# Second-choice result loads on ScalarE's DMA queue, first-choice loads on SyncE's

## The chip, the cores and the metric

The kernel runs on 1 core of one Trainium2 chip. The metric is the device time of one execution in microseconds, taken as the median of several runs. All times of the profile are of one profiled execution and count from the start of its span.

## What is computed

Two blocks over x of 8 x 512 tokens x 256 features, each an adaptively modulated attention followed by an adaptively modulated feed-forward part. The last of the four parts is a mixture of experts: every token picks 2 of 8 experts, each expert takes at most 1280 slots, and the two results of a token are added with its two shares. Cut to that part:

```python
top_p, top_i = jax.lax.top_k(probs, K)                      # K = 2
top_p = top_p / jnp.sum(top_p, axis=-1, keepdims=True)
...
fc1 = jax.nn.gelu(jnp.einsum('ech,ehf->ecf', xt, moe_w1))   # E = 8 experts, cap 1280
fc2 = jnp.einsum('ecf,efh->ech', fc1, moe_w2).reshape(T, H)
weighted = fc2 * padded_probs[:, None]
moe_out = jnp.zeros((N, H)).at[padded_tid].add(weighted)
return h1 + moe_out.reshape(S, B, H)
...
x = x + gb * _L1_ffn_ref(h, ...)
```

## The kernel before

Everything is written by hand in one stream per engine with semaphores between them; nothing is scheduled by a planner. `layer0`, `layer1` and `cross` compute the first three parts with x held in SBUF; `moe` is the last part and the only one that the change touches.

In `moe`, 40 chunks of 256 slots go through the experts. For each chunk GpSimd gathers rows (L2153), TensorE turns them and does both products (L2360, L2374, L2386), ScalarE applies the gain and the Gelu (L2313, L2321), VectorE copies the result out of PSUM (L2257), and GpSimd scatters it by indirect DMA (L2161) into the DRAM tensor `expert_parts` (`c.parts`). This tensor has two halves of 4096 rows of 256 floats: the results of the tokens' first choices, and those of the second.

After the last scatter the two halves are put together, one batch b = 0..7 of 512 tokens at a time:

- SyncE waits until the base sums are done and all four scatter semaphores are full (L2132 to L2135), and then issues 16 loads back to back, in the order y(0), rows(0), y(1), rows(1), ...: L2137 loads the first choices' results of batch b into `c.y[:, b]`, L2138 the second choices' into `rows(b)`, which lies in `c.prob` for b < 4 and in `c.probT` from there. Each is 512 KB, 128 partitions x 4 runs of 1 KB. Both raise `landed{b}`; batches 6 and 7 share one semaphore.
- Behind them in SyncE's stream stand 8 waits on `finished`, each with one store of a batch to the output (L2141).
- ScalarE waits for `landed{b}` and scales y(b) by the first share, in 4 ACTIVATEs (L2330), raising `scaled`.
- VectorE's `summed(b)` waits for `scaled` and adds rows(b) times the second share, 4 instructions at L2275; `finished(b)` multiplies by the gate (L2282) and adds to x (L2283). They are written in the order summed(0), summed(1), finished(0), summed(2), finished(1), ...

ScalarE's stream has no DMA in it anywhere in the program, and between its last Gelu (L2321) and its first scaling (L2330) it has nothing to do but wait.

Of the kernel before, what the change touches and what calls it, by code (L numbers as in the profile page):

```python
# [23 lines left out]
B = 8  # L24
T = 512
# [83 lines left out]
def mod_rows(c, l, name):  # L109

    at = CHUNK[name] * D
    return c.mod_dram[l, :, at:at + D].partition_broadcast(P)
# [1938 lines left out]
TT = CHUNK_T // P  # L2051
CHUNKS = CAP // CHUNK_T
ALL_CHUNKS = E * CHUNKS
# [4 lines left out]
BUFS = 4  # L2058
# [4 lines left out]
def moe(c, d, start, out):  # L2063

    nc = c.nc
    s = c.s
    with ExitStack() as st:
# [37 lines left out]
        def rows(b):  # L2105
            half = c.prob if b < B // 2 else c.probT
            at = 2 * (b % (B // 2))
            return half[:, at:at + 2, :].rearrange("p i (t n) -> p (i t) n", n=D)
# [4 lines left out]
        def tokens(dram, b):  # L2113
            return dram[b * T:(b + 1) * T, :].rearrange("(t p) n -> p t n", p=P)
# [7 lines left out]
        @block.sync  # L2122
        def _(sp):
            sp.dma_start(gate[:, :, :], mod_rows(c, 1, "gb")).then_inc(s["moe_loaded"], 16)
            for e in range(E):
                z = e % 2
                if e >= 2:
                    sp.wait_ge(s["down_full"], CHUNKS * (e - 1))
                sp.dma_start(w1[z][:, :, :], d["we1"][e].rearrange("(k p) n -> p k n", p=P))\
                  .then_inc(s[("expert_weights0", "expert_weights1")[z]], 16)  # L2130
                sp.dma_start(w2[z][:, :, :], d["we2"][e].rearrange("(k p) n -> p k n", p=P))\
                  .then_inc(s[("expert_weights0", "expert_weights1")[z]], 16)  # L2132
            sp.wait_ge(s["base_done"], B)
            for z in range(BUFS):
                sp.wait_ge(s[("scattered0", "scattered1", "scattered2", "scattered3")[z]], 16 * TT * (ALL_CHUNKS // BUFS))  # L2135
            for b in range(B):
                sp.dma_start(c.y[:, b], tokens(c.parts[0:B * T, :], b)).then_inc(s[f"landed{min(b, B - 2)}"], 16)  # L2137
                sp.dma_start(rows(b), tokens(c.parts[B * T:2 * B * T, :], b)).then_inc(s[f"landed{min(b, B - 2)}"], 16)  # L2138
            for b in range(B):
                sp.wait_ge(s["finished"], b + 1)  # L2140
                sp.dma_start(out[b].rearrange("(t p) n -> p t n", p=P), c.x[:, b]).then_inc(s["stored"], 16)  # L2141
            sp.wait_ge(s["stored"], 16 * B)
# [149 lines left out]
        @block.scalar  # L2292
        def _(act):
            act.wait_ge(s["logits_shifted"], 1)
            nc.scalar.activation(lg[:, :, :], lg[:, :, :], ACT.Exp).then_inc(s["logits_exped"], 1)

            act.wait_ge(s["lows_ready"], 1)
            for x in range(1, PAIRS // PIECE, 2):
                if x >= 2:
                    act.wait_ge(s["pairs_used"], x - 1)  # L2300
                for m in range(PIECE):
                    k = PIECE * x + m
                    ins = nc.scalar.activation(lohot[1][:, m, :], c.lows[:, 0, :], ACT.Abs, bias=minus_low[:, k:k + 1],  # L2303
                                               scale=1.0)
                ins.then_inc(s["low_away"], 1)
                act.wait_ge(s["low_away"], x // 2 + 1)
                nc.scalar.activation(lohot[1][:, :, :], lohot[1][:, :, :], ACT.Relu, bias=c.ones[:, 0:1], scale=-1.0)\  # L2307
                  .then_inc(s["low_hots"], 1)

            def gain(j):  # L2310
                act.wait_ge(s["in_full"], j + 1)
                for k in range(KD):
                    ins = nc.scalar.activation(inT[j % 2][:, k, :], IN[j % 2][:, k * CHUNK_T:(k + 1) * CHUNK_T],  # L2313
                                               ACT.Identity, bias=c.gains[:, 2 + k:3 + k], scale=c.gains[:, k:k + 1])
                ins.then_inc(s["in_out"], 1)

            gain(0)
            for j in range(ALL_CHUNKS):
                for i in range(2):
                    act.wait_ge(s["up_full"], 2 * j + i + 1)  # L2320
                    nc.scalar.activation(gT[j % 2][:, 2 * i:2 * i + 2, :],  # L2321
                                         UP[(2 * j + i) % 4].rearrange("p (m t) -> p m t", m=2),
                                         ACT.Gelu_apprx_tanh).then_inc(s["up_out"], 1)
                if j + 1 < ALL_CHUNKS:
                    gain(j + 1)
            for b in range(B):
                act.wait_ge(s[f"landed{min(b, B - 2)}"], 32 if b < B - 2 else 64)
                for t in range(NT):
                    k = b * NT + t
                    ins = nc.scalar.activation(c.y[:, b, t, :], c.y[:, b, t, :], ACT.Identity, bias=c.zero[:, :],  # L2330
                                               scale=share[:, 0, k:k + 1])
                ins.then_inc(s["scaled"], 1)
# [157 lines left out]
```

## Time and profile before

| | us |
|---|---|
| median of 3 runs | 3152.18 |
| lowest, highest | 3151.83, 3153.38 |
| the profiled execution's own time | 3159.02 |
| its span | 3157.3 |

| engine | busy us, share of the span |
|---|---|
| PE | 2904.5, 92% |
| DVE | 1646.8, 52% |
| ACT | 1403.8, 44% |
| POOL | 836.2, 26% |

The span runs from the first to the last instruction or transfer. PE's share is an average over the whole program; the last stretch, from 3107.7 us on, has no matmul in it, and there the shares of the table say nothing. Rows marked SPq are the DMA issues in SyncE's stream: start, and the time until the stream could go on.

### The profile page before, as it was taken

The numbers are of one execution on the slowest core, as the hardware profiler recorded it, in microseconds if no ns is written. First come the engines' busy times: TensorE is split into PE (matmuls) and PEld (weight loads), VectorE is DVE, ScalarE is ACT, GpSimd is POOL, SyncE is SP. The second block draws the span as 40 slices with busy tenths as digits, with TensorE's granted clock in tenths as the row PEclk, the third lists the DMA queues.
The fourth block names the chain that finished last, engine by engine and source line by source line (L and its number), as shares of the span: only waits on it lengthen the run. The fifth ranks groups of instructions, "written<-read, shape, count | busy, mean of one in ns | idle before, by whom it ended". The sixth has DMA issues, their size and how long they took to land. (4 is left out here: it accounts for less than half of the span.)

```text
span 3157.3 us, 53117 instructions
## 1 busy us (share of the span) xinstructions
PE 2904.5 (92%) x20820; PEld 1968.8 (62%) x20820; DVE 1646.8 (52%) x5006; ACT 1403.8 (44%) x3081; POOL 836.2 (26%) x831
## 2 busy tenths in 40 slices
PE   6889999878999999999999999999999688899993
PEld 3566666654666757576666666665656444478883
DVE  4667776645555544544444444445554488631114
ACT  3666666632535444444444444534444124132222
POOL 1001111113333332332323222233333311025551
PEclk8999999999999999999999999999999899789997
DMA  4111111004000000000010000000000000112325
GB/s 139 18 19 20 18 20 20 8 3 164 8 4 10 6 16 30 1 1 1 13 33 1 1 1 5 28 14 11 6 6 11 11 1 27 53 41 79 73 83 186
DMA packets 66232, 93.95 MB, mean 30 GB/s; under 512 B 9971, under 2 KB 52982, under 8 KB 64944
## 3 DMA queue, kind: packets, MB, share of 16 engines
q1 hardware_dynamic: 58304, 74.24, 8.0%
q0 software_dynamic: 7680, 16.32, 2.0%
q8 instruction: 166, 2.72, 0.4%
q14 instruction: 82, 0.67, 0.1%
HBM read 59.31 MB, written 27.36 MB: 27 GB/s over the span
## 5 line engine op out<-in xcount | busy, mean ns | idle before, releaser
L1343 PE MATMUL bank<-h2T,w 128*128 128x512 f32 x1024 | 478.9, 606 | 5.3 <-ACT gT L1281 3.7
L1381 PE MATMUL bank<-w,gT 128*128 128x256 f32 x2048 | 465.9, 381 | 0.0
L1381 PEld LDWEIGHTS bank<-w,gT 128*128 128x128 f32 x2048 | 379.3, 190 | 49.7 <-issue 0.5
L1018 POOL TENSOR_TENSOR prob<-prob,rsum 128x512 f32<-128x512 f32 (+1 forms) x256 | 237.7, 949 | 591.0 <-DVE rsum L1165 591.0
L1343 PEld LDWEIGHTS bank<-h2T,w 128*128 128x128 f32 x1024 | 182.2, 190 | 224.0 <-issue 173.7
L1281 ACT ACTIVATE gT<-bank,vec 128x512 f32<-128x512 f32 x256 | 175.1, 687 | 285.6 <-PE bank L1343 284.2
L583 ACT ACTIVATE y<-y,least 128x128 f32<-128x128 f32 (+3 forms) x512 | 252.2, 555 | 52.4 <-DVE least L463 52.3
L463 DVE CUSTOM_DVE_ANT_0 y<-bank,mask 128x128 f32<-128x128 f32 (+3 forms) x512 | 223.9, 486 | 71.9 <-PE bank L680 71.0
L1171 DVE COPY probT<-bank 128x1024 f32<-128x1024 f32 (+1 forms) x128 | 139.3, 1088 | 226.7 <-PE bank L1397 226.7
L1142 DVE CUSTOM_DVE_ANT_0 prob<-bank,mask 128x256 f32<-128x256 f32 (+1 forms) x512 | 164.3, 386 | 168.1 <-PE bank L1333 168.1
L1253 ACT ACTIVATE prob<-prob,least 128x256 f32<-128x256 f32 (+1 forms) x512 | 239.9, 473 | 15.8 <-DVE least L1142 15.5
L1316 PE MATMUL bank<-wtok,hT 128*128 128x512 f32 x512 | 225.0, 592 | 1.3 <-ACT hT L1244 1.3
L696 PE MATMUL bank<-ident,y 128*128 128x128 f32 x1280 | 182.7, 279 | 47.0 <-DVE probT L268 33.4
L696 PEld LDWEIGHTS bank<-ident,y 128*128 128x128 f32 x1280 | 142.5, 142 | 111.6 <-issue 90.0
L1298 ACT COPY aoT<-bank 128x512 f32<-128x512 f32 x32 | 18.8, 587 | 368.5 <-PE bank L1409 368.5
L1262 ACT COPY tok<-bank 128x384 f32<-128x384 f32 x128 | 61.3, 479 | 238.5 <-PE bank L1316 238.5
L1316 PEld LDWEIGHTS bank<-wtok,hT 128*128 128x128 f32 x512 | 97.2, 190 | 110.2 <-issue 108.6
L268 DVE COPY probT<-bank 128x512 f32<-128x512 f32 (+1 forms) x160 | 101.4, 633 | 119.4 <-PE bank L696 119.4
L2257 DVE COPY yout<-bank 128x512 f32<-128x512 f32 x40 | 27.7, 692 | 258.8 <-PE bank L2386 258.8
L1074 DVE TENSOR_SCALAR xn<-y,mv,rstd 128x256 f32<-128x256 f32 x256 | 133.0, 582 | 52.2 <-POOL rstd L999 52.2
L2374 PE MATMUL bank<-inT,we 128*128 128x256 f32 x640 | 146.5, 382 | 3.3 <-ACT inT L2313 3.3
L2386 PE MATMUL bank<-we,score 128*128 128x256 f32 x640 | 144.6, 379 | 0.0
(313 smaller groups left out, 5010.7 us busy)
## 6 DMA issues: line engine op xcount, KB each, us to landing
w<-in_W SPq DMA_DIRECT2D x8, 1024.0 KB, 5.9
expert_parts<-zeros SPq DMA_DIRECT2D x8, 1024.0 KB, 16.2
we<-in_we SPq DMA_DIRECT2D x16, 512.0 KB
rows<-modulation SPq DMA_DIRECT2D x40, 128.0 KB, 2.9
x<-in_x SPq DMA_DIRECT2D x8, 512.0 KB, 6.3
prob<-score SPq DMA_DIRECT2D x64, 64.0 KB, 2.4
probT<-score SPq DMA_DIRECT2D x64, 64.0 KB, 2.4
token_rows<-rows_normed SPq DMA_DIRECT2D x4, 1024.0 KB, 4.4
```

Of the source, the lines that this page charges most:

```text
L463: nc.vector.tensor_tensor_reduce(out=prob[:, j, FROM[tile]:FROM[tile] + width], in0=S[:, j, at:at + width], in1=mask[:, T - width:T], scal ...
L583: ins = nc.scalar.activation(one, one, ACT.Exp, bias=least[:, n % 2, tile, j:j + 1], scale=-1.0)
L696: ins = nc.tensor.transpose(H[at % 2][:, col:col + P], prob[:, j0 + j, src:src + P], c.ident[:, :])
L1018: nc.gpsimd.tensor_tensor(two, two, rsum[:, at:at + 2].unsqueeze(2).to_broadcast([P, 2, width]), ALU.mult).then_inc(s["probs"], 1)
L1142: nc.vector.tensor_tensor_reduce(out=prob[:, at, from_col(q):PAIR], in0=S[:, j, off:off + width], in1=mask[:, from_col(q):PAIR], scale=1.0 ...
L1253: nc.scalar.activation(one, one, ACT.Exp, bias=least[:, at:at + 1], scale=-1.0, accum_out=sums[:, at:at + 1]).then_inc(s["exped"], 1)
L1281: nc.scalar.activation(gT[:, m, :], M[m % 2][:, :], ACT.Gelu, bias=v[:, 4 * KD + m:4 * KD + m + 1]).then_inc(s["gelu_done"], 1)
L1316: ins = nc.tensor.matmul(S[:, t, :], hT[:, k, 1 + t * P:1 + (t + 1) * P], wtok[:, k, :], start=(k == 0), stop=(k == KD - 1))
L1343: ins = nc.tensor.matmul(M[m % 2][:, :], w1[:, k, m * P:(m + 1) * P], h2T[:, k, :], start=(k == 0), stop=(k == KD - 1))
L1381: ins = nc.tensor.matmul(M[i][:, (t % 2) * D:(t % 2 + 1) * D], gT[:, m, t * P:(t + 1) * P], w2[:, m, :], start=(m == 0), stop=(m == MF - 1))
L2374: ins = nc.tensor.matmul(UP[(2 * j + i) % 4][:, (m % 2) * CHUNK_T:(m % 2 + 1) * CHUNK_T], w1[e % 2][:, k, m * P:(m + 1) * P], inT[j % 2][: ...
L2386: ins = nc.tensor.matmul(DOWN[j % 2][:, t * D:(t + 1) * D], gT[j % 2][:, k, t * P:(t + 1) * P], w2[e % 2][:, k, :], start=(k == 0), stop=( ...
```

## The change

The loads of the second choices' results leave SyncE's stream and go into ScalarE's, behind its last Gelu and ahead of its first scaling, with waits on the same four scatter semaphores. SyncE keeps the 8 loads of the first choices' results. Sizes, addresses, semaphores raised and the order within each kind stay.

```diff
             for b in range(B):
                 sp.dma_start(c.y[:, b], tokens(c.parts[0:B * T, :], b)).then_inc(s[f"landed{min(b, B - 2)}"], 16)
-                sp.dma_start(rows(b), tokens(c.parts[B * T:2 * B * T, :], b)).then_inc(s[f"landed{min(b, B - 2)}"], 16)
             for b in range(B):
                 sp.wait_ge(s["finished"], b + 1)
                 sp.dma_start(out[b].rearrange("(t p) n -> p t n", p=P), c.x[:, b]).then_inc(s["stored"], 16)
...
                 if j + 1 < ALL_CHUNKS:
                     gain(j + 1)
+            for z in range(BUFS):
+                act.wait_ge(s[("scattered0", "scattered1", "scattered2", "scattered3")[z]],
+                            16 * TT * (ALL_CHUNKS // BUFS))
+            for b in range(B):
+                nc.scalar.dma_start(rows(b), tokens(c.parts[B * T:2 * B * T, :], b))\
+                  .then_inc(s[f"landed{min(b, B - 2)}"], 16)
             for b in range(B):
                 act.wait_ge(s[f"landed{min(b, B - 2)}"], 32 if b < B - 2 else 64)
```

ScalarE's stream at the end of the program, in the kernel before (`score` is the buffer that Gelu writes, `y` what is scaled):

```order
L2313 ACTIVATE inT<-bank,moe_gain 128x256 x2
L2321 ACTIVATE score<-bank 128x512 x2
L2330 ACTIVATE y<-y,zero_moe,share 128x256 x32
L2067 UNCONDITIONAL_BRANCH
```

The same place in the changed kernel:

```order
L2312 ACTIVATE inT<-bank,moe_gain 128x256 x2
L2320 ACTIVATE score<-bank 128x512 x2
L2329 DMA prob<-expert_parts 128x4x256 x4
L2329 DMA probT<-expert_parts 128x4x256 x4
L2335 ACTIVATE y<-y,zero_moe,share 128x256 x32
L2067 UNCONDITIONAL_BRANCH
```

All eight DMAs stand ahead of the first of the 32 scalings, which before had none ahead of them.

SyncE's stream at the end of the program, as a difference:

```order
-L2137 DMA y<-expert_parts 128x4x256
-L2138 DMA prob<-expert_parts 128x4x256
...
-L2137 DMA y<-expert_parts 128x4x256
-L2138 DMA probT<-expert_parts 128x4x256
-L2141 DMA out_x<-x 128x4x256 x8
+L2137 DMA y<-expert_parts 128x4x256 x8
+L2140 DMA out_x<-x 128x4x256 x8
 L2067 UNCONDITIONAL_BRANCH
```

The eight loads of `prob` and `probT` are gone from between the loads of `y`; the stores stand behind them as before.

## Rows read from the trace of the kernel before

**Rows 1.** Chain that ended last, in order of time: start us, us, what.

```profile
3100.77 6.92 PE bank L2386 x32
...
3110.53 2.43 DMA expert_parts<-yout,dst_row
...
3114.55 6.90 DMA prob<-expert_parts
...
3121.48 2.08 ACT y L2330 x4
...
3123.59 1.67 DVE y L2275 x4
```

**Rows 2.** Timeline of DVE at the end: start us, us, ..., count [idle before, releaser].

```profile
3120.65 1.67 DVE L2275 SCALAR_TENSOR_TENSOR y<-prob,share,y 128x256 f32<-128x256 f32 x4 [12.18 <-ACT y L2330]
3123.59 1.67 DVE L2275 SCALAR_TENSOR_TENSOR y<-prob,share,y 128x256 f32<-128x256 f32 x4 [1.26 <-ACT y L2330]
...
3127.57 1.67 DVE L2275 SCALAR_TENSOR_TENSOR y<-prob,share,y 128x256 f32<-128x256 f32 x4
...
3147.47 1.67 DVE L2275 SCALAR_TENSOR_TENSOR y<-probT,share,y 128x256 f32<-128x256 f32 x4
...
3152.70 1.23 DVE L2283 TENSOR_TENSOR x<-x,y 128x1024 f32<-128x1024 f32 x1
```

**Rows 3.** Timeline of ACT at the end.

```profile
3100.81 0.60 ACT L2321 ACTIVATE score<-bank 128x512 f32<-128x512 f32 x1 [1.13 <-PE bank L2374]
3118.47 2.08 ACT L2330 ACTIVATE y<-y,zero_moe,share 128x256 f32<-128x256 f32 x4 [17.06 <-DMA prob<-expert_parts]
3121.48 2.07 ACT L2330 ACTIVATE y<-y,zero_moe,share 128x256 f32<-128x256 f32 x4 [0.94 <-DMA prob<-expert_parts]
3124.49 2.08 ACT L2330 ACTIVATE y<-y,zero_moe,share 128x256 f32<-128x256 f32 x4 [0.94 <-DMA prob<-expert_parts]
...
3140.27 4.04 ACT L2330 ACTIVATE y<-y,zero_moe,share 128x256 f32<-128x256 f32 x8 [3.74 <-DMA probT<-expert_parts]
```

**Rows 4.** Timeline of SyncE's DMA issues at the end.

```profile
3113.04 0.37 SPq L2137 DMA_DIRECT2D y<-expert_parts  x1
3113.45 0.51 SPq L2138 DMA_DIRECT2D prob<-expert_parts  x1
...
3115.10 0.61 SPq L2137 DMA_DIRECT2D y<-expert_parts  x1
3115.76 1.36 SPq L2138 DMA_DIRECT2D prob<-expert_parts  x1
3117.16 1.42 SPq L2137 DMA_DIRECT2D y<-expert_parts  x1
3118.62 1.42 SPq L2138 DMA_DIRECT2D prob<-expert_parts  x1
3120.08 1.42 SPq L2137 DMA_DIRECT2D y<-expert_parts  x1
...
3123.28 1.42 SPq L2137 DMA_DIRECT2D y<-expert_parts  x1
...
3131.51 1.42 SPq L2138 DMA_DIRECT2D probT<-expert_parts  x1
3133.26 21.06 SPq L2141 DMA_DIRECT2D out_x<-x  x8
```

**Rows 5.** Stretches: A:B length, busy PE PEld DVE ACT POOL, PEclk, DMA share, GB/s.

```profile
3115.00:3125.00 10.00, 0.00 (x0) 0.00 (x0) 3.09 (x8) 4.66 (x10) 0.00 (x0) 0.50 1.09 353
3139.00:3140.00 1.00, 0.00 (x0) 0.00 (x0) 1.00 (x3) 0.00 (x0) 0.00 (x0) 0.50 1.09 386
```

## The prediction

> **What bounds the kernel now.** I read the chain that ended last first, because the change touches only the last 50 us, in which the page's overall shares say nothing. The chain [rows 1] leaves TensorE after its last products (3100.77 + 6.92 = 3107.7 us), goes over the last scatter, which lands at 3110.53 + 2.43 = 3113.0, then over a load that lands 6.9 us after its issue, one ScalarE batch of 2.08 us, and from 3123.59 on it is VectorE.
>
> The timeline of VectorE [rows 2] tells why it stays there. Its first batch of L2275 starts at 3120.65, then it waits 1.26 us for ScalarE, and from 3123.59 it never waits again: batches follow at 3127.57 and so on to 3147.47, that is (3147.47 - 3123.59) / 6 = 3.98 us each, and the last instruction ends at 3152.70 + 1.23 = 3153.93. The last store then closes the span at 3157.3. So the end is **the start of VectorE's second batch plus 3157.3 - 3123.59 = 33.7 us**, and whatever comes later than VectorE wants it doesn't count. The question is only what the change does to that 3123.59.
>
> The timeline of ScalarE [rows 3] gives the step before: its batches start at 3118.47, 3121.48 and 3124.49, each as the pair of loads of its batch has landed, 3.01 us apart. Two loads are 1.05 MB, and 1.05 MB / 3.01 us = 348 GB/s; the stretch of ten us beside it reads 353 GB/s at a DMA share of 1.09 [rows 5]. The 16 DMA engines are full, from the first pair to the last (the last two batches are released at 3140.27).
>
> The fourth view is SyncE's issues [rows 4], and here lies the price. The first five take 0.37 to 0.61 us. From the sixth on an issue takes 1.36 or 1.42 us: the stream is held. By what, is read by putting the ends beside the landings. The seventh issue ends at 3117.16 + 1.42 = 3118.58, just after the second load's landing released ScalarE (3118.47); the ninth at 3120.08 + 1.42 = 3121.50, after the fourth load's (3121.48); the eleventh at 3123.28 + 1.42 = 3124.70, after the sixth load's (3124.49). Three times the issue of load n ends within 0.2 us of the landing of load n - 5: **one queue takes five of these loads, and the sixth holds the issuing stream until the first is out**.
>
> **The change part by part.**
>
> *SyncE's eight issues removed.* They cost nothing now: SyncE has only the stores behind them, the first of which goes out at 3133.26 and none of which but the last is on the path. The last waits for VectorE at 3153.93. Gain 0.
>
> *The loads' data.* The same 8.4 MB over the same 16 engines, which are full. If the two queues share them evenly, y(b) and rows(b) move side by side at half speed each, and the pair is complete when it was before: 3118.4, 3121.4, 3124.5. The second load's issue comes 0.4 us earlier, but the engines start with y(0) as before and have work since then, so that brings nothing. The trace has no two queues of this kind side by side, so this is bounded: from below by the fastest stretch, 386 GB/s [rows 5], by which the three pairs up to 3124.7 would take 9.0 x 353/386 = 8.2 us, 0.8 less; from above I allow the half microsecond that one issue takes (0.51), if the issues of the two queues hinder each other. I take 0, since the stretch that holds loads alone, as here, is the one with 353 GB/s.
>
> *ScalarE's eight issues added.* This is the term. They are in order ahead of the first scaling, and ScalarE's own scalings, then VectorE, stand behind them. Five go out at 0.4 to 0.6 us each, as on SyncE, until about 3115.7. The sixth (b = 5) ends when rows(0) is out, the seventh when rows(1) is, the eighth when rows(2) is. With even sharing rows(2) is out when the third pair is, by the eleventh issue of [rows 4] at **3124.70**. Until then ScalarE can't scale, though batches 0 and 1 have lain there since 3118.4 and 3121.4. Before, it began at 3118.47. The lateness is 6.2 us at the first batch.
>
> *What of it reaches the end.* ScalarE then has three batches waiting and does two in 4.04 us (the row of eight in [rows 3]). VectorE's first batch follows the first of them and fits in between (1.67 against some 2 us). Its second starts at 3124.70 + 0.04 + 4.04 + 0.03 = 3128.8: 0.04 from the end of an issue to the next instruction, as from 3118.58 to 3118.62 on SyncE [rows 4], and 0.03 from ScalarE's end to VectorE's start, as from 3121.48 + 2.08 = 3123.56 to 3123.59 [rows 2, 3]. The change to VectorE's second batch is 3128.8 - 3123.59 = **+5.2 us**. From there on VectorE is never short: ScalarE needs 2.02 us for a batch and VectorE 3.98, and the last pair is released at 3140.3 where VectorE wants batch 6 at 3128.8 + 5 x 3.98 = 3148.7. So nothing of it is won back, nor is more lost.
>
> *ScalarE's new waits on the scatters* have nothing behind them that was earlier: the last Gelu ends at 3101.4 and the scatter lands at 3113.0, when SyncE begins too. 0.
>
> Sum: span 3157.3 + 5.2 = 3162.5, the profiled execution's own time 3159.02 + 5.2 = 3164.2. This one execution is 6.8 us above the median of the runs; the tail is the same in kind, so I put the difference on the median: 3152.2 + 5.2 = **3157.4 us**. With the bounds of the load rate and of the hindrance: 3156.6 to 3157.9; with an issue cost on ScalarE that no row shows, up to double SyncE's 0.51, another 0.5: 3158.4.
>
> **Where the notes bear on it.** The Trainium skill, page "DMA: Bandwidth & Descriptors", section "Issuing engines are not separate DMA queues", says that several issuing engines share the same 16 DMA engines and that spreading issues only saves issue time. By that rule the landings stay as they are, as the full share of the DMA engines also suggests, and the change would be worth 0 at worst; it has no term for an issuing stream that is held by its full queue, which SyncE's rows of 1.42 us show. The section "Queues, rings and completion order" of the same page gives each queue a ring of its own on each engine, which would speak against the first rival below. No run here shows it so far. The page "Perfetto Trace Analysis", section "DMA Instruction — HWDGE (DVE, Sync)", says that the block that writes descriptors is shared and locked while it is in use, which would speak for the third; nothing of the sum rests on these.
>
> **The rivals.**
>
> 1. *The five places are shared by the two queues.* Then ScalarE's eighth issue is the fifteenth or sixteenth of all and ends as that one did, 3131.51 + 1.42 = 3132.93. The second batch starts at 3132.93 + 4.11 = 3137.0, **+13.4 us: 3165.6**, slower by 0.43%. For it: all that is seen is that loads wait for loads to leave the same 16 engines. Against: the stream that was held is always SyncE's, so the trace can't tell. It decides as soon as ScalarE's last issue ends after 3125.8, 1.1 us behind the forecast's 3124.7; then the loss passes 6.3 us. Chance 0.17.
>
> 2. *ScalarE isn't held*: its queue takes eight loads, or it passes a full queue. The eight issues then take 0.37 + 7 x 0.55 = 4.2 us and end at 3117.3, before the first pair is there (3118.4). **±0: 3152.2**. Against: SyncE is held, and ScalarE's instructions too go in order. Chance 0.09.
>
> 3. *One queue goes ahead of the other at issuing.* In the extreme SyncE puts out its eight first, the last when y(2) has landed at 3120.04, and ScalarE's eight start then; its first three share the engines with SyncE's last ones, three pairs at 3.0 us, until about 3129 to 3130, where the eighth issue ends. **About +10: 3162**. Chance 0.05.
>
> 4. *The loads get faster by two queues.* Even then VectorE can't start its second batch before two pairs have landed and two were scaled; with 386 GB/s and ScalarE not held the second pair comes 0.6 us earlier. This gives 0.6, not the 6.3 us that 0.2% are. Chance of faster 0.02 with all that I haven't thought of.
>
> The forecast has the rest, 0.67.
>
> **How the numbers follow.** 0.2% of 3152.2 is 6.3 us, about what a measurement of this kernel can tell from no change, and my +5.2 lies 1.1 us under it. Of the forecast's 0.67 I give 0.11 to being over that bound (a stream held until all of a load has left the slowest engine, dearer issues, and the measurement). Slower: 0.11 + 0.17 + 0.05 = 0.33. Same: 0.56 + 0.09 = 0.65. Faster: 0.02. The range takes in the forecast, with a run's spread of about 1.5 us around its bounds, and the rivals 1 and 3: 3153.0 to 3166.5; it leaves out the case of no wait, faster, and small tails, about 0.14. The forecast's own range is 3155.5 to 3159.5.
>
> **What would show it.** In the changed kernel's timeline of ScalarE: eight issues behind the last Gelu, the first five at about 0.5 us, the sixth to eighth some 3 us each (a queue at half speed), the last ending near 3124.7; then eight or more scalings in one row without idle time. VectorE's first batch near 3126.8 instead of 3120.65, its second near 3128.8, then 3.98 us each. SyncE's sixth to eighth issue held likewise, and DMA at about 350 GB/s from 3115 on. Issues on ScalarE that end at 3133 show rival 1, those that end at 3117 rival 2. Wrong altogether would be a landing of the third pair that isn't at 3124.5: then sharing isn't even or the rate has changed.

## The result and the profile after

| | before | changed |
|---|---|---|
| median of 9 runs, us | 3153.38 | 3160.89 |
| lowest, highest | 3151.83, 3156.51 | 3156.97, 3164.99 |
| profiled execution, own time | 3159.02 | 3164.99 |
| its span | 3157.3 | 3163.3 |

The ratio of the times is **1.0022, with a 95% interval of 1.0013 to 1.0030**: the change costs 7 us, between 4 and 9.5. In a later set the same kernel came out at 1.0029 (1.0018 to 1.0041). The forecast was +5.2 us, or 3157.4 us, and the way is right. The measured 3160.89 us lies inside the stated range (3153.0 to 3166.5) but above the forecast's own (3155.5 to 3159.5). The bound of 0.2% that I had set for "slower" lies inside the interval, and the medians are just over it. One of the ten runs of e7 further down took 3508.94 us at a granted clock of 0.832 instead of 0.965 to 0.971, and its ratio leaves that run out.

Since each execution reaches the last part a few microseconds earlier or later, I count from the start of SyncE's first load of the last part (3113.04 us in the trace of before, 3111.24 in that of after), with a plus sign. The end of the span is +44.3 before and +52.1 after: 7.8 us lie between the first load and the end, all of the loss.

The chain that ended last, of the changed kernel, answers to [rows 1] (start us, us, what):

```profile
3108.74 2.42 DMA expert_parts<-yout,dst_row
...
3111.26 0.45 ACTq L2329
...
3111.74 0.53 ACTq L2329
...
3112.29 0.53 ACTq L2329
...
3112.85 1.28 ACTq L2329
...
3114.16 2.31 ACTq L2329
...
3116.49 2.88 ACTq L2329
...
3119.40 2.89 ACTq L2329
...
3122.32 2.89 ACTq L2329
...
3125.26 4.04 ACT y L2335 x8
...
3129.32 1.67 DVE y L2274 x4
```

Where a load and its landing stood, eight issues of ScalarE stand (ACTq). The first three take half a microsecond, the fourth 1.28, the fifth 2.31, and the last three 2.9 each. Then come two batches of scaling in one piece, as for the forecast, and VectorE's second batch. The timelines of ScalarE and VectorE answer to [rows 3] and [rows 2]:

```profile
3125.26 11.90 ACT L2335 ACTIVATE y<-y,zero_moe,share 128x256 f32<-128x256 f32 x24 [25.65 <-issue]
3138.71 4.04 ACT L2335 ACTIVATE y<-y,zero_moe,share 128x256 f32<-128x256 f32 x8 [1.55 <-DMA probT<-expert_parts]
```

```profile
3127.44 1.67 DVE L2274 SCALAR_TENSOR_TENSOR y<-prob,share,y 128x256 f32<-128x256 f32 x4 [20.76 <-ACT y L2335]
3129.32 1.67 DVE L2274 SCALAR_TENSOR_TENSOR y<-prob,share,y 128x256 f32<-128x256 f32 x4 [0.21 <-ACT y L2335]
...
3133.31 1.66 DVE L2274 SCALAR_TENSOR_TENSOR y<-prob,share,y 128x256 f32<-128x256 f32 x4
...
3158.42 1.23 DVE L2282 TENSOR_TENSOR x<-x,y 128x1024 f32<-128x1024 f32 x1
```

ScalarE did 24 scalings, six batches, without a gap, because their loads had long been in. Its idle time is put down to "issue": the profile knows no releaser for it, since what the engine waited for stood in its own stream. VectorE's second batch is at +18.1 instead of +10.55. In the timeline of SyncE's issues, which answers to [rows 4], its eight loads take 13.20 us, and the last of them alone 2.88 us: they are held in the same way. The stretch of ten microseconds that answers to [rows 5] shows that the loads run at the same rate, 354 GB/s against 353:

```profile
3111.24 13.20 SPq L2137 DMA_DIRECT2D y<-expert_parts  x8
...
3121.57 2.88 SPq L2137 DMA_DIRECT2D y<-expert_parts  x1
...
3133.42 26.63 SPq L2140 DMA_DIRECT2D out_x<-x  x8
```

```profile
3115.00:3125.00 10.00, 0.00 (x0) 0.00 (x0) 0.00 (x0) 0.00 (x0) 0.00 (x0) 0.50 1.10 354
```

The trace also tells when each load landed, as the time from the start of its issue. For the third load of ScalarE (rows(2), issued at 3112.29), and for the same load in e6 further down (issued at 3114.55):

```profile
L2329 ACTq DMA_DIRECT2D prob<-expert_parts x1: 528/528/528, 3112.3 to 3112.3; - x1
...
DMA to landing us min/median/max: 11.2/11.2/11.2
```

```profile
L2330 ACTq DMA_DIRECT2D prob<-expert_parts x1: 528/528/528, 3114.6 to 3114.6; - x1
...
DMA to landing us min/median/max: 10.9/10.9/10.9
```

Read in this way, load by load, SyncE's first four loads of the changed kernel land at +5.0, +8.1, +11.1 and +14.1, and ScalarE's at +5.6, +9.2, +12.2 and +15.2. SyncE's load of a batch is up to 1.1 us ahead of ScalarE's load of the same batch, and the third pair is complete at +12.2 instead of +11.45 (+12.0 in e5).

### The profile page after: what moved, and what is told of

The parts are those of the page before. It is cut to its first block and busy times, and to the rows that moved or that the text cites. A ratio compares the mean times of both kernels' runs of the same rounds, so it can differ in the third digit from the quotient of the medians.

```text
span 3163.3 us, 53119 instructions
## 1 busy us (share of the span) xinstructions
PE 2905.4 (92%) x20820; PEld 1969.7 (62%) x20820; DVE 1646.5 (52%) x5006; ACT 1402.7 (44%) x3081; POOL 834.7 (26%) x831
```

## The experiments

Theory A: ScalarE's stream is held at its own full queue, and everything behind it is late by that. Theory B: two queues bring the pairs later or out of step. C and D, P and N and the rest are named in the expectations. Times "at +" are from each run's own trace:

| run | ScalarE's last issue ends | first scaling | VectorE's second batch | end of span |
|---|---|---|---|---|
| before | - | 5.43 | 10.55 | 44.3 |
| changed | 13.97 | 14.02 | 18.08 | 52.1 |
| e5, changed again | 13.83 | 13.89 | 17.96 | 51.9 |
| e1, four ahead | (held in none) | 5.50 | 10.99 | 45.0 |
| e9, six ahead | 8.02 (the sixth) | 8.07 | 13.10 | 47.0 |
| e2, late scaling | - | 11.48 | 15.56 | 49.2 |
| e3, queue used before | 11.99 | 12.04 | 16.12 | 50.1 |
| e6, the same again | 11.96 | 12.01 | 16.08 | 50.1 |
| e12, queue half used | 11.90 | 11.95 | 16.02 | 50.0 |
| e4, half loads | 16.77 | 16.82 | 20.89 | 54.8 |
| e7, runs of 4 KB | 4.58 | 5.34 | 10.14 | 44.1 |
| e8, add on GpSimd | - | 5.46 | 10.57 | 53.4 |
| e10, first batch early | - | 5.46 | 10.57 | 44.3 |
| e11, early and 4 KB | - | 4.95 | 9.98 | 43.1 |

### Fewer loads ahead of the scaling (e1, e9)

```diff
-            for b in range(B):
-                nc.scalar.dma_start(rows(b), ...)
+            for b in range(4):                  # e9: 6
+                load_rows(b)
             for b in range(B):
                 act.wait_ge(s[f"landed{min(b, B - 2)}"], 32 if b < B - 2 else 64)
                 ...
                 ins.then_inc(s["scaled"], 1)
+                if b + 4 < B:                   # e9: b + 6
+                    load_rows(b + 4)
```

> ScalarE issues rows(0) to rows(3) ahead of its first scaling and each rows(b + 4) behind the scaling of batch b; SyncE as in the changed kernel. Theory A (the loss is ScalarE's stream held at its full queue): in the changed kernel the first three issues took 0.5 us and the fourth 1.3, so the stream is free 2.9 us after the first issue, before the first pair is in at 6.0. ScalarE starts at 6.0 and VectorE's second batch 11.8 us after the first issue (second pair at 9.6, a batch of 2.1), against 18.1 in the changed kernel and 10.55 in the one before: 1.2 us slower than before, about 3154.5 us. Theory B (the loss is that two queues bring the pairs later or out of step): the loss stays at 5 us or more, about 3159 us.

Measured: 1.0006 of before (0.9997 to 1.0016); VectorE's second batch at +10.99, the end at +45.0. The same two queues carry the same loads, and 7.1 of the 7.8 us are gone. For theory B 0.7 us are left at the end. ScalarE's timeline:

```profile
3115.77 2.51 ACTq L2329 DMA_DIRECT2D prob<-expert_parts  x4
3121.25 0.60 ACT L2338 ACTIVATE y<-y,zero_moe,share 128x256 f32<-128x256 f32 x1 [17.14 <-DMA prob<-expert_parts]
3121.26 0.37 ACTq L2329 DMA_DIRECT2D probT<-expert_parts  x1
...
3124.64 0.60 ACT L2338 ACTIVATE y<-y,zero_moe,share 128x256 f32<-128x256 f32 x1 [1.31 <-DMA prob<-expert_parts]
```

Four issues take 2.51 us, the first scaling waits for a landing again, and the fifth issue, given out later, takes 0.37 us where it took 2.31. The pairs are in at +5.50, +8.89 and (from the next row of the same kind) +11.90, where before they were in at 5.43, 8.44 and 11.45: from the second on they come 0.45 us later. I had expected VectorE's second batch 1.2 us later than before; it came 0.44 us later.

> As the run with four loads ahead of ScalarE's first scaling, with six. In the changed kernel's trace the sixth issue ended 8.1 us after the first. If the loss is the hold and nothing else, the first scaling starts at 8.15 us, VectorE's second batch at 8.15 + 4.1 = 12.2 to 12.3 (four ahead: 10.99, eight: 18.0), and the end lies 46.2 us after the first issue (44.95 and 52.0). If two queues cost something of their own with more loads in them, later than that.

Measured: 1.0012 (1.0002 to 1.0021). The hold is as forecast, the first scaling at +8.07. But VectorE's second batch is at +13.10 instead of 12.25, and I had overlooked why: the seventh load stands behind batch 0's scaling and ahead of batch 1's, and it is held too. The chain shows it: the second batch's scaling begins at 3124.65, 2.92 us after the first's at 3121.73, with 0.85 us of "issue" before it. The eighth load, ahead of batch 2's scaling, is held as long and costs nothing more, since VectorE goes on to its third batch without idle time:

```profile
3121.83 2.77 ACTq L2329 DMA_DIRECT2D probT<-expert_parts  x1
...
3124.75 2.77 ACTq L2329 DMA_DIRECT2D probT<-expert_parts  x1
```

```profile
3126.76 1.67 DVE L2274 SCALAR_TENSOR_TENSOR y<-prob,share,y 128x256 f32<-128x256 f32 x4 [1.17 <-ACT y L2338]
...
3130.75 1.67 DVE L2274 SCALAR_TENSOR_TENSOR y<-prob,share,y 128x256 f32<-128x256 f32 x4
```

A held issue costs when the work behind it is on the path. Four, six and eight ahead give an end at +45.0, +47.0 and +52: with six, four issues are held as in the changed kernel, but only three of them ahead of the second batch's scaling.

### The sum without a second queue (e2)

```diff
+            act.wait_ge(s["landed2"], 32)
             for b in range(B):
                 act.wait_ge(s[f"landed{min(b, B - 2)}"], 32 if b < B - 2 else 64)
```

> The kernel before, all loads on SyncE, but ScalarE's first scaling also waits for the third pair of loads, the moment at which I had forecast that the held stream would be free. This is the forecast's sum without a second queue. Theory A: the first scaling starts 11.5 us after the first issue instead of 5.4, VectorE's second batch 15.5 to 15.6 us after it instead of 10.55, end +5.0 us: about 3158.3 us. If part of the lateness were made good further down, less than +4.

Measured: 1.0018 (1.0009 to 1.0028), about 5.7 us; second batch at +15.56, end at +49.2, that is +5.0. All that the forecast said of what lies behind ScalarE's start holds to a tenth of a microsecond: a start 6.05 us later is 5.0 us at VectorE's second batch and 5.0 at the end, and none of it is won back.

### What ScalarE's queue had carried before (e3, e5, e6, e12)

```diff
-            sp.dma_start(gate[:, :, :], mod_rows(c, 1, "gb")).then_inc(s["moe_loaded"], 16)
...
             nc.scalar.activation(lg[:, :, :], lg[:, :, :], ACT.Exp).then_inc(s["logits_exped"], 1)
+            act.wait_ge(s["rows_stored"], 16 * NT)
+            nc.scalar.dma_start(gate[:, :, :], mod_rows(c, 1, "gb")).then_inc(s["moe_loaded"], 16)
```

In e12 ScalarE loads `gate[:, 0:4]` and SyncE `gate[:, 4:8]`.

> The changed kernel, with the load of the gates (L2124) moved from SyncE to ScalarE early in the last part, so that ScalarE's queue has carried a load before. Theory C (the 1.3 us by which ScalarE's first load starts moving behind SyncE's is the price of a queue's first use): rows(0) lands 4.3 to 4.6 us after its issue instead of 5.6, the last issue ends 0.6 us earlier or more, and VectorE's second batch comes at 17.4 or before. Theory D (it comes from both streams issuing at the same moment, or from the queue itself): as in the changed kernel, shortest landing 5.6 us, second batch at 18.1.

> The changed kernel itself once more, beside the next one. In its first trace ScalarE's last issue ended 13.95 us after its first, about 1.4 us after the third pair's landing, while in the kernel with ScalarE's queue used before it ended after 11.98 us. If that is a property of the kernel (a queue that had not been used before), it is 13.9 to 14.0 again and VectorE's second batch at 18.1; if it varies from execution to execution, anything from 11.9 to 14.0.

> The kernel with the gates' load on ScalarE's queue once more. If the earlier use of the queue is what matters: last issue 12.0 us after the first, VectorE's second batch at 16.1, and a median 2 us below the changed kernel's of the same call. If it varies: no such difference in the medians.

> The changed kernel with half of the gates' load (four of the eight batches, 512 runs of 1 KB) on ScalarE's queue and half on SyncE's. With all of it (1024 runs) on ScalarE's queue the last issue ended 12.0 us after the first in two executions, without it 13.8 and 14.0. If any earlier use of the queue is what helps: 12.0 again. If it hangs on how far the queue has been filled before, by runs: another value, most simply 13.9 with the short issue not yet reached, since in the kernel with all of it the one issue that took 1.1 us instead of 2.9 was the very last.

Measured: without an earlier load on ScalarE's queue the last issue ends at +13.97 and +13.83, with one at +11.99, +11.96 and +11.90, whether it was 512 or 1024 runs. Five executions fall into two groups with 1.8 us between them, so it is most likely a property of the kernel and not of the execution. Nearly all of the gain, 1.6 us, is in one issue. The chain of e6:

```profile
3116.17 2.20 ACTq L2330
...
3118.40 2.84 ACTq L2330
...
3121.26 2.89 ACTq L2330
...
3124.19 1.27 ACTq L2330
```

The last issue takes 1.27 us where the changed kernel's takes 2.89; those ahead of it are alike to a quarter of a microsecond. SyncE's queue is a counterexample to the plain rule "used before, so more room": it had carried loads in the whole program, and in the same trace its eighth issue takes 2.92 us.

```profile
3123.84 2.92 SPq L2136 DMA_DIRECT2D y<-expert_parts  x1
```

What I set out with in e3, that ScalarE's first load starts to move late because it is the queue's first use, is refuted by its landing: 5.6 us after the issue in the changed kernel and in e5, 5.6 in e3, and 5.5 in e6 and e12. VectorE's second batch came early, as that theory asked, but not by its mechanism. Nor is it the data: rows(2) lands at +12.0 in e5 and at +12.0, +12.0 and +11.9 in e3, e6 and e12. (The "1.4 us after the third pair's landing" in e5's expectation is 1.7 by the landing of +12.2.)

The times of e5 and e6, side by side, are 1.0029 (1.0018 to 1.0041) and 1.0025 (1.0014 to 1.0036), that of e12 1.0021 (1.0011 to 1.0031), and the only time of e3 is 3161.28 us. The median of e6 was to be 2 us below that of e5 and is 0.75 us above it: 1.8 us of 3155 are too little for the times, and this part rests on the traces alone. Why the last issue ends earlier was not found.

### What fills a queue (e4, e7)

```diff
             for b in range(B):
-                nc.scalar.dma_start(rows(b), ...)
+                for h in range(2):              # 256 KB each
+                    nc.scalar.dma_start(rows(b)[:, 2 * h:2 * h + 2, :], ...)
```

> The changed kernel, with each of ScalarE's eight loads cut into two of 256 KB, half the runs of 1 KB each; all 16 ahead of the first scaling. Theory P (a queue's places are counted in runs, some 4.4 loads of 512 runs): the last issue ends when 3.6 of 8 batches are out, as in the changed kernel, 14.0 us after the first issue, second batch at 18.1. Theory N (they are counted in loads, 4.4): 11.6 of 16 halves have to be out, 5.8 batches at 2.9 us, and the last issue ends about 20.3 us after the first, second batch at 24.4, 6.3 us slower than the changed kernel.

Measured: one run, 3168.25 us. Neither: the last issue ends at +16.77, between 14.0 and 20.3. Nine halves go out before one is held, against four whole loads. (The fourth whole load takes 0.97 to 1.28 us, but a fourth load takes 0.98 in e7 too, where nothing is held.)

```profile
3116.33 0.49 ACTq L2330
...
3116.86 2.91 ACTq L2330
...
3119.80 1.43 ACTq L2330
```

So it isn't the number of loads alone, as the ninth goes out unheld and in 0.49 us. Nor is it their runs alone. By their landings, the eighth half (+16.2) is in at +16.77 and the ninth (+17.8) a third of its way, which leaves some 7.6 halves in the queue. In the changed kernel, at +13.97, rows(2) is in (+12.2) and rows(3) (+15.2) a little over half of its way, which leaves 4.4 loads. The same number of runs would be 8.8 halves, the same number of loads 4.4. A load that fills the queue by its runs and by some fixed amount beside them fits both: an estimate from two points, no more.

```diff
-            by_place = c.token_rows.rearrange("(b t p) n -> t p b n", t=NT, p=P)
+            by_place = c.token_rows.rearrange("(b p t) n -> t p b n", t=NT, p=P)
...
-            nc.gpsimd.iota(c.value[:, :], pattern=[[P, PAIRS]], base=1, channel_multiplier=1,
+            nc.gpsimd.iota(c.value[:, :], pattern=[[T, PAIRS // NT], [1, NT]], base=1, channel_multiplier=NT,
...
-            return dram[b * T:(b + 1) * T, :].rearrange("(t p) n -> p t n", p=P)
+            return dram[b * T:(b + 1) * T, :].rearrange("(p t) n -> p t n", p=P)
```

> The changed kernel with the rows of both DRAM tensors stored in another order (partition before tile), so that a load of 512 KB is 128 runs of 4 KB instead of 512 runs of 1 KB; the gathers and scatters follow by the slot table. Theory P (places are counted in runs): eight loads need 64 runs on each engine where the eight of 1 KB runs needed 256, nothing is held, ScalarE's issues end 4.2 us after the first, its scalings start with the first pair at about 5.4, VectorE's second batch at 10.5 to 11.0, end within 1 us of the kernel before. Theory N (counted in loads or bytes): the last issue ends after 12 to 14 us, end 5 to 7.5 us behind.

Measured: 1.0000 of before (0.999 to 1.001), end at +44.1. This is the changed kernel, with all eight loads ahead of the scaling, the same bytes and the same number of loads; what differs is that the runs are four times as long, and where the rows lie in DRAM:

```profile
3106.90 4.44 SPq L2137 DMA_DIRECT2D y<-expert_parts  x8
3106.91 2.33 ACTq L2329 DMA_DIRECT2D prob<-expert_parts  x4
3109.27 2.21 ACTq L2329 DMA_DIRECT2D probT<-expert_parts  x4
3112.24 2.07 ACT L2335 ACTIVATE y<-y,zero_moe,share 128x256 f32<-128x256 f32 x4 [16.99 <-DMA prob<-expert_parts]
```

The eight issues of ScalarE take 4.54 us, the longest of them this one:

```profile
3108.26 0.98 ACTq L2329 DMA_DIRECT2D prob<-expert_parts  x1
```

No issue is held, and the end is where it was before the change. At the end of the eighth issue, +4.58, none of ScalarE's loads has landed (the first does at +5.3), so it is not the faster transfer that makes the room. With e4 this shows that neither bytes nor the number of loads alone fills a queue of this kind, and that the number of runs counts for most. The stretch 3110 to 3120 of the same trace has 413 GB/s instead of 354, and the pairs come 2.6 us apart instead of 3.0. A part of what is won back is this, so that e7 alone doesn't show that two queues cost nothing: against e11, which has the same runs on one queue, its first two pairs come 0.4 and 0.2 us later (+5.34 and +8.03 against +4.95 and +7.80).

### Towards a faster end (e8, e10, e11)

```diff
-                nc.vector.tensor_tensor(c.x[:, b], c.x[:, b], c.y[:, b], ALU.add).then_inc(s["finished"], 1)
...  in GpSimd's stream, behind the last scatter
+            for b in range(B):
+                pool.wait_ge(s["multiplied"], b + 1)
+                nc.gpsimd.tensor_tensor(c.x[:, b], c.x[:, b], c.y[:, b], ALU.add).then_inc(s["finished"], 1)
```

> The kernel before, with the last addition of each batch (L2283) on GpSimd, which has no work there. If VectorE's 3.98 us a batch is what sets the end, as the forecast has it: VectorE needs 2.8 us a batch, the pairs of loads at 3.0 us take over, the last two pairs are released 27.2 us after the first issue, two scalings 4.0, sum 1.7, gate 1.2, GpSimd's addition about 1.9 (twice the 0.95 us of its 128x512 operation), store 3.4: end at 39.5 us instead of 44.3, 4.8 us faster, about 0.15%. If GpSimd and VectorE hinder each other: no gain.

Measured: 1.0034 (1.0020 to 1.0048), end at +53.4, slower by 9.1 us. The timeline, all engines:

```profile
3116.29 1.67 DVE L2279 SCALAR_TENSOR_TENSOR y<-prob,share,y 128x256 f32<-128x256 f32 x4 [1.25 <-ACT y L2334]
...
3119.25 2.34 POOL L2177 TENSOR_TENSOR x<-x,y 128x1024 f32<-128x1024 f32 x1 [15.05 <-DVE y L2286]
3119.30 3.76 DVE L2279 SCALAR_TENSOR_TENSOR y<-prob,share,y 128x256 f32<-128x256 f32 x4 [0.20 <-ACT y L2334]
```

VectorE's four instructions take 1.67 us alone and 3.76 beside GpSimd's addition, and one of the four takes the difference:

```profile
L2279 DVE SCALAR_TENSOR_TENSOR y<-prob,share,y x4: 473/473/2574, 3119.3 to 3122.6; 128x256 f32<-128x256 f32 x4
```

It stands still for nearly the length of the other. A batch is 4.8 us on VectorE instead of 3.98, although the addition is gone from it. That is 2.7 us at VectorE's last instruction, which ends at +43.6 instead of +40.9; the other 6.4 us lie behind it, where GpSimd's last two additions and the last store now stand. An addition on GpSimd takes 2.34 to 2.52 us beside VectorE's batch; I had expected 1.9. The Trainium skill, page "SBUF — State Buffer", section "SBUF: two separate sides", describes this: the two engines share a pair of ports by an exclusive lock that is held for a whole instruction. The trace agrees: GpSimd's addition starts first, at 3119.25, and VectorE's four instructions from 3119.30 on take 3.76 instead of 1.67 us.

```diff
             dve.wait_ge(s["base_done"], B)
-            for b in range(B + 1):
-                if b < B:
-                    summed(b)
-                if b:
-                    finished(b - 1)
+            summed(0)                           # waits tile by tile for ScalarE
+            finished(0)
+            for b in range(1, B + 1):
+                if b < B:
+                    summed(b)
+                if b > 1:
+                    finished(b - 1)
```

> The kernel before, all loads on SyncE. VectorE takes batch 0 tile by tile as ScalarE scales it, and gates and adds it at once, in the time in which it waits for batch 1. If VectorE's work from its second batch on sets the end: summed(1) starts at about 10.7 instead of 10.55 us after the first issue but has finished(0) behind it, 2.45 us; the end comes 2.2 us earlier, 42.1 us after the first issue, about 0.07% of the whole, less than the times can tell.

> The same with runs of 4 KB, all 16 loads on SyncE. The first pair is in at 5.3 us after the first issue, the second 2.6 us later instead of 3.0, so VectorE isn't held by loads: it starts at about 5.9, its second batch at 10.5, the end 41.9 to 42.1 us after the first issue. SyncE's 16 issues end after 16 x 0.55 = 8.8 us and none takes over 0.6 us, if a queue's places are counted in runs (128 runs of 4 KB for a load where there were 512).

Measured: e10 1.0002 (0.9993 to 1.0011), end at +44.3, nothing won. VectorE had batch 0 wholly done by its second batch at +10.57, as meant, and then stood idle:

```profile
3119.62 1.67 DVE L2276 SCALAR_TENSOR_TENSOR y<-prob,share,y 128x256 f32<-128x256 f32 x4
3123.60 1.67 DVE L2276 SCALAR_TENSOR_TENSOR y<-prob,share,y 128x256 f32<-128x256 f32 x4 [2.31 <-ACT y L2333]
```

The 2.3 us went into a wait for batch 2, whose loads are in at +12.4 here (+11.45 before). I had checked that batch 1 comes in time and not batch 2. e11 gives back a part: its end is at +43.1 (1.2 us ahead of the kernel before), where I had expected +41.9 to +42.1, and 0.9997 (0.9988 to 1.0006) in the times. In the trace it is the only one well ahead of both kernels, and for the times no different from the one before. "VectorE isn't held by loads" failed here too: batch 2's pair comes 3.5 us after batch 1's and not 2.6, and VectorE waits 1.75 us for it.

```profile
3120.13 2.07 ACT L2333 ACTIVATE y<-y,zero_moe,share 128x256 f32<-128x256 f32 x4 [1.41 <-DMA prob<-expert_parts]
...
3122.24 1.67 DVE L2276 SCALAR_TENSOR_TENSOR y<-prob,share,y 128x256 f32<-128x256 f32 x4 [1.75 <-ACT y L2333]
```

Its 16 issues on one queue took 0.34 to 0.71 us, save for the last with 1.06. My "none over 0.6" was a little low; none is held as with runs of 1 KB.

## Why the prediction was right, and where it was short

- *Where the time is set.* Right: the start of VectorE's second batch plus a constant. The constant was 33.7 us before and 3163.3 - 3129.32 = 34.0 after.
- *SyncE's issues cost nothing.* Right: ScalarE's last issue, not SyncE's stores, is on the path.
- *The data come as before.* Nearly. The rate is the same, but sharing isn't even: SyncE's loads land up to 1.1 us ahead of ScalarE's of the same batch, and the third pair is in at +12.2 (+12.0 in e5) instead of +11.45. The prediction had called a third pair that isn't at 3124.5 the sign of being wrong, and had allowed half a microsecond where 0.5 to 0.8 were measured. In e1, where this alone is left, it costs 0.45 us from the second pair on and 0.7 at the end. Why SyncE's loads are ahead was not found.
- *ScalarE's stream is held until its eighth load is out.* The mechanism is right: e1 takes the hold away and leaves 0.7 of 7.8 us, and e2 makes 5.0 us of loss without a second queue. Its size was short. **The term that failed is "the eighth issue ends when rows(2) is out, at 3124.70", +11.7**: measured were +13.97 and +13.83. What failed in it is the rule that the issue of load n ends with the landing of load n - 5. It holds on the one queue of the kernel before and for none of the changed kernel's last three issues on either queue:

  | issue | ends | load n - 5 landed | load n - 4 landed |
  |---|---|---|---|
  | before, SyncE's 6th, 7th, 8th | 4.1, 5.5, 7.0 | 3.9, 5.4, 6.9 | 5.4, 6.9, 8.4 |
  | changed, ScalarE's 6th, 7th, 8th | 8.1, 11.1, 14.0 | 5.6, 9.2, 12.2 | 9.2, 12.2, 15.2 |
  | changed, SyncE's 6th, 7th, 8th | 7.3, 10.3, 13.2 | 5.0, 8.1, 11.1 | 8.1, 11.1, 14.1 |
  | e6, ScalarE's 6th, 7th, 8th | 7.7, 10.7, 12.0 | 5.5, 8.9, 12.0 | 8.9, 12.0, 14.9 |

  In the changed kernel an issue ends 1.7 to 2.5 us behind the landing of load n - 5 and 0.8 to 1.2 us ahead of that of load n - 4. On one queue, where loads land 1.5 us apart, "with n - 5" and "1.3 to 1.4 us ahead of n - 4" are the same moment, and the rows of the kernel before couldn't tell them apart. Read in the second way they would have given 11.45 + 3.0 - 1.35 = 13.1 for the eighth issue, and a loss of 5.2 + 1.4 = 6.6 us: an estimate from the rows of before, which no run has tested by itself. Only the eighth issue of e3, e6 and e12 ends with the landing of rows(2), as forecast, and those ahead of it do not. The fifth issue, for which the forecast had 0.4 to 0.6 us, took 2.31. (Of SyncE's issues before, the tenth and the twelfth took 1.70 and 2.33 us, not 1.36 or 1.42 as the prediction has it for all from the sixth on; they too end within 0.3 us of the landing of load n - 5.) In the forecast's own terms the difference at the eighth issue is 0.8 us for the later rows(2) and 1.5 us for the rule: 5.2 + 0.8 + 1.5 = 7.5, and VectorE's second batch came 18.08 - 10.55 = 7.5 us later.
- *ScalarE then needs 4.04 us for two batches, and nothing is won back.* Right to 0.1 us, by the changed kernel and by e2.
- *Rival 1, places shared by both queues*, asked for a last issue that ends at 3132.93, +19.9. It ended at +14.0. That is later than the +12.8 from which the rival was to be decided, and the loss passed 6.3 us as said there, but for another reason. What refutes the rival are the loads in flight: at +5.3 both engines had given out five each and only one, SyncE's first at +5.0, had landed, so nine were in flight where the rival has five. The Trainium skill, page "DMA: Bandwidth & Descriptors", section "Queues, rings and completion order", gives each queue a ring of its own on each engine; the trace agrees, with nine in flight.
- *Rival 2, ScalarE not held*, is refuted by the rows of 2.9 us.
- *Rival 3, one queue ahead of the other.* Its number, about 3162, came nearer to the measured 3160.9 than the forecast's 3157.4, but not by its mechanism: SyncE's last issue ends at +13.2 and ScalarE's at +14.0, where the rival has SyncE's eight out before ScalarE's. A mild form, SyncE's loads 1.1 us ahead, is in the trace.
- *Rival 4, faster loads by two queues*: no, 354 against 353 GB/s.
- *Spreading issues over engines.* The Trainium skill, page "DMA: Bandwidth & Descriptors", section "Issuing engines are not separate DMA queues", says that spreading issues over engines only saves issue time. The trace agrees for the data, whose rate doesn't change (354 against 353 GB/s). For the kernel it was not so: it lost 7 us, because the second issuing engine had work of its own behind its issues.
- *The chances.* 0.65 on "within 0.2%" and 0.33 on slower: the sum lay 1.1 us under the bound, and its largest term was carried over from one queue to two in tenths of a microsecond. A margin that thin called for more on the slower side. That the measured time lies in the stated range is owed to the room made in it for rivals 1 and 3, and not to the sum, which is 2.3 us short; another 1.2 us of the miss come from the median of before, 3152.2 us in three runs and 3153.4 in nine.

## What to carry to other kernels

A DMA issue is cheap only as long as its queue has room; a stream of issues longer than that holds the engine that gives them out, at the pace of the transfers, so put them on an engine with nothing urgent behind them, or give them out a few at a time between the work, as e1 does. How many fit is to be read from the issue durations in the trace: here four to five loads of 512 runs, and at least eight if the same bytes are in runs of 4 KB. A rule read from one queue need not hold for two, since each queue then moves at half the pace (loads 3.0 us apart instead of 1.5). Before putting idle time to use (e10), check the next arrival too, and before giving work to an idle engine (e8), what it shares with the busy one.

## What was not expected of the hardware

- When ScalarE's queue had carried a load earlier, 512 or 1024 runs of 1 KB, the last of its eight issues took 1.25 to 1.27 us instead of 2.89, in three executions against two; SyncE's eighth, on a queue used all along, took 2.88 to 2.92 in all five. The cause is open.
- Of two loads issued 0.02 us apart on two queues SyncE's landed 0.6 us earlier, and 1.1 us earlier from the second batch on.
- Beside a TENSOR_TENSOR of 128x1024 on GpSimd, which takes 2.34 to 2.52 us, VectorE's four instructions of a batch take 3.76 instead of 1.67 us.
- Loads of 512 KB in runs of 4 KB move at 413 GB/s (e7), in runs of 1 KB at 353 to 354 (before and changed).
